# Layers 0, 2 and 3 of a four-layer cross-attention network: projections as 64-row halves in two rounds, values once per quad, a lag of eight waves

## The chip, the core and the metric

The kernel runs on one core of a Trainium2 chip. The metric is device time in microseconds, the median of three runs. The core has TensorE (matrix products, with a queue of its own for weight loads), VectorE, ScalarE, GpSimd and SyncE, which issues most DMAs here. Engines run side by side, each through its own instruction list in order, and wait for one another by semaphores.

## What is computed

x holds 128 rows of 256. Four layers follow, each of cross attention, self attention and a feed-forward part, each added to x. The change touches the cross attention of layers 0, 2 and 3, which has this form (layer 2 has no mask and, like layer 3, an output product):

```python
q = _split_heads(hidden_states @ q_w.T + q_b)      # 128 queries, 16 heads of 16
k = _split_heads(context @ k_w.T + k_b)            # 12544 keys
v = _split_heads(context @ v_w.T + v_b)
scores = jnp.einsum('bhqd,bhkd->bhqk', q, k) / jnp.sqrt(jnp.float32(HD))
scores = jnp.where(mask, -jnp.inf, scores)
probs = jax.nn.softmax(scores, axis=-1)
ctx = jnp.einsum('bhqk,bhkd->bhqd', probs, v)
```

Everything is float32 up to rounding; products that must be exact enough use split high and low parts.

## The kernel before

`cross_attention_turned` (L645) takes the 12544 keys in NB = 14 **blocks** of 896 keys (7 tiles of 128). The softmax is computed block by block with a running maximum. The 16 heads of a block are handled as four **quads** of four heads. A quad takes four **waves**, so a block has 16 waves; I call the four waves of one quad a group and number them 0 to 3 by `g % 4`. One loop over g runs in the lists of TensorE, ScalarE and VectorE; `u = g - LAG` is the wave that has come to its scores when wave g is at its maxima.

What each wave does on TensorE:

- `maxima` (L904 to L917): two products, one for each half of the array's rows (`rows_of(0)` is rows 0 on, `rows_of(1)` rows 64 on), 448 keys wide, into two banks of a ring of three, `m_bank`. VectorE's `top_of` (L1151) reduces each to a row maximum.
- `scores` (L919 to L930): 4 or 3 key tiles, each as two products in the two row halves, into two banks of a second ring of three, `s_bank`. ScalarE's `exps` (L1053) makes `prob` of them, one instruction a bank: four tiles (128x512) or three (128x384).
- `values` (L944 to L955), every second wave, for half a quad: per key tile four products, each with all 128 rows and 32 columns of the array, side by side. They are float32, and each is two instructions in the trace. They sum up in the bank `p_oT`.
- `project_next` (L897), in the other waves: one of the 8 **items** of the next block. Items 0 to 3 are keys (six products of 448 columns each, three split parts times two chunks of the contraction), items 4 to 6 are values for two tiles (twelve products of 256 columns), item 7 for one tile (six). All use all 128 rows, and all go to the one bank `p_proj`. ScalarE copies an item out (`evacuate`, L1037 for keys, L1043 for values), VectorE makes the low part of the keys (`k_low`, L1111).
- `turn_q` once per group: two 128x128 turns of the queries with the new maxima, which VectorE has split in `split_top` (L1175, L1177) out of `raise_top` (L1165). ScalarE copies them to `q_sub` (L1059).
- `turn_out` once per block: four 128x128 turns of the block's result, after ScalarE's `copy_out` (L1071) of 128x512; VectorE adds it up (L1184).

So TensorE's order in a group is maxima, scores, values | maxima, scores, projection, turn of the queries | maxima, scores, values | maxima, scores, projection. In numbers of a block: 16 pairs of maxima, 56 pairs of score products, 56 rounds of four value products, 24 products of 448 and 42 of 256 columns, 8 turns of queries, 4 of the result.

SyncE loads the context of block b + 2 and, once all four key items of block b + 1 are split, rearranges these keys by 24 DMAs, six for each quad, into `k_stack` (L767), where maxima and scores read them. GpSimd splits a loaded context into its parts (L837, and L839 by subtraction). Block 0's projections stand before the loop. The last block has none to make, and after the last maxima LAG more waves of scores, then values and turns, follow before the layer's end.

`keep_busy` (L1240) issues products that nobody uses. The functions that the diff touches, and what calls them:

## Time and profile before

| | us |
|---|---|
| median of 3 runs | 2401.51 |
| lowest, highest | 2388.33, 2405.67 |
| the profiled execution | 2400.72 |
| its span on the core | 2398.9 |
| first to last maxima: layer 0, layer 2, layer 3 | 26.6 to 469.4, 1303.7 to 1741.7, 1831.9 to 2270.0 |

The profile is of one execution. The page lists busy time by engine, the clock granted to TensorE in tenths of the full one, and groups of instructions. The timeline lists runs of like instructions: start, time from the first start to the last end, engine, line, tiles, shape, count. As TensorE's products are pipelined, a run's time is the gaps between the starts and the length of its last product (0.27 us for 128 columns, 0.37 for 448); what follows can start before that end. "128*32" is the part of the array that an instruction uses, rows times columns.

### The profile page before, as it was taken

How to read it: one execution, taken by the hardware profiler on the slowest of the kernel's cores; microseconds unless marked ns; L12 is line 12 of the kernel's file. 1: busy time of each engine (PE TensorE's matmuls, PEld its weight loads, DVE VectorE, ACT ScalarE, POOL GpSimd, SP SyncE). 2: the span in 40 equal slices, each digit the busy share in tenths (PEclk: the TensorE clock that was granted, in tenths of full speed). 3: DMA queues.
4: the chain of work that ended last, by engine and by line, in shares of the span. 5: the costliest groups of instructions: out<-in, count | busy, mean ns of one | idle time of the engine just before them, and what ended most of it. 6: DMA issues, size and time to landing. Idle time of an engine off the chain costs nothing. (4 is left out here: it accounts for less than half of the span.)

```text
span 2398.9 us, 68493 instructions
## 1 busy us (share of the span) xinstructions
PE 2254.4 (94%) x26863; PEld 1884.1 (79%) x26863; DVE 1594.7 (66%) x3621; ACT 1504.3 (63%) x3041; POOL 413.5 (17%) x356
## 2 busy tenths in 40 slices
PE   7999999988999999999778999999977999999968
PEld 6888888777788887887756888888866888888758
DVE  6777777635777777777564777777735777777632
ACT  3666666624788787888524666666633666666611
POOL 3222122002221212210002212222003221122000
PEclk9999999989999999999898999999978999999979
DMA  7667776365344354441154766666516667766335
GB/s 148 118 120 121 125 116 122 54 215 155 100 125 113 106 131 102 116 122 41 46 178 98 148 110 116 115 117 116 82 50 141 121 121 126 127 115 119 57 119 190
DMA packets 152460, 279.62 MB, mean 117 GB/s; under 512 B 32829, under 2 KB 72078, under 8 KB 152218
## 3 DMA queue, kind: packets, MB, share of 16 engines
q1 hardware_dynamic: 148842, 272.18, 55.0%
q10 hardware_dynamic: 3376, 4.03, 0.6%
...
## 5 line engine op out<-in xcount | busy, mean ns | idle before, releaser
L1151 DVE TENSOR_REDUCE L3x_tops<-L3x_m_bank 128x1 f32<-128x448 f32 x448 | 262.6, 619 | 124.5 <-PE L3x_m_bank L915 122.4
L1151 DVE TENSOR_REDUCE L0x_tops<-L0x_m_bank 128x1 f32<-128x448 f32 x448 | 262.7, 619 | 121.8 <-PE L0x_m_bank L915 119.6
L1151 DVE TENSOR_REDUCE L2x_tops<-L2x_m_bank 128x1 f32<-128x448 f32 x448 | 262.7, 619 | 118.4 <-PE L2x_m_bank L915 116.3
L559 DVE CUSTOM_DVE_ANT_0 L1x_p_s<-L1x_p_s,L1x_mask,L1x_neg_max 128x512 f32<-128x512 f32 (+1 forms) x400 | 288.7, 742 | 55.7 <-PE L1x_p_s L320 53.1
L452 ACT ACTIVATE L1x_prob<-L1x_p_s,L1x_neg_max 128x512 f32<-128x512 f32 (+1 forms) x400 | 275.0, 687 | 68.2 <-DVE L1x_neg_max L559 66.2
L1053 ACT ACTIVATE L2x_prob<-L2x_s_bank 128x512 f32<-128x512 f32 x448 | 219.6, 542 | 90.9 <-PE L2x_s_bank L926 89.7
L1053 ACT ACTIVATE L0x_prob<-L0x_s_bank 128x512 f32<-128x512 f32 x448 | 219.6, 542 | 89.9 <-PE L0x_s_bank L926 88.7
L1053 ACT ACTIVATE L3x_prob<-L3x_s_bank 128x512 f32<-128x512 f32 x448 | 219.6, 542 | 87.6 <-PE L3x_s_bank L926 86.1
L329 PE MATMUL L1x_p_t<-net_ident,L1x_prob 128*128 128x128 f32 x1568 | 239.4, 274 | 13.8 <-ACT L1x_probT L174 11.4
L329 PEld LDWEIGHTS L1x_p_t<-net_ident,L1x_prob 128*128 128x128 f32 x1568 | 191.8, 140 | 56.9 <-ACT L1x_probT L174 23.6
L320 PE MATMUL L1x_p_s<-L1x_k_stack,L1x_q_stack 96*128 96x512 f32 (+1 forms) x400 | 181.6, 456 | 1.8 <-DVE L1x_q_stack L542 1.8
L174 ACT COPY L1x_probT<-L1x_p_t 128x512 f32<-128x512 f32 (+1 forms) x300 | 172.7, 576 | 1.6 <-PE L1x_p_t L329 1.3
L926 PEld LDWEIGHTS L2x_s_bank<-L2x_q_sub,L2x_k_stack 50*128 50x128 f32 x1568 | 122.8, 189 | 9.6 <-ACT L2x_prob L1053 6.2
L926 PEld LDWEIGHTS L0x_s_bank<-L0x_q_sub,L0x_k_stack 52*128 52x128 f32 x1568 | 122.5, 188 | 9.4 <-ACT L0x_prob L1053 6.3
L926 PEld LDWEIGHTS L3x_s_bank<-L3x_q_sub,L3x_k_stack 52*128 52x128 f32 x1568 | 121.5, 186 | 9.2 <-ACT L3x_prob L1053 6.1
L926 PE MATMUL L2x_s_bank<-L2x_q_sub,L2x_k_stack 50*128 50x128 f32 x1568 | 116.3, 261 | 3.1 <-ACT L2x_prob L1053 2.9
L926 PE MATMUL L0x_s_bank<-L0x_q_sub,L0x_k_stack 52*128 52x128 f32 x1568 | 115.9, 260 | 3.1 <-ACT L0x_prob L1053 2.9
L926 PE MATMUL L3x_s_bank<-L3x_q_sub,L3x_k_stack 52*128 52x128 f32 x1568 | 114.7, 258 | 3.1 <-ACT L3x_prob L1053 2.9
L915 PE MATMUL L3x_m_bank<-L3x_k_stack,L3x_q_max 52*128 52x448 f32 x448 | 109.1, 467 | 7.3 <-DMA L3x_k_stack<-L3x_kT 5.7
L915 PE MATMUL L0x_m_bank<-L0x_k_stack,L0x_q_max 52*128 52x448 f32 x448 | 109.4, 469 | 4.8 <-DMA L0x_k_stack<-L0x_kT 3.2
L915 PE MATMUL L2x_m_bank<-L2x_k_stack,L2x_q_max 50*128 50x448 f32 x448 | 108.7, 466 | 3.3 <-DMA L2x_k_stack<-L2x_kT 1.6
L953 PE MATMUL L2x_p_oT<-L2x_prob,L2x_v 128*32 128x128 f32 x3136 | 111.6, 281 | 0.0
...
## 6 DMA issues: line engine op xcount, KB each, us to landing
L0x_k_stack<-L0x_kT SPq DMA_DIRECT2D x333, 112.0 KB, 4.1
L2x_k_stack<-L2x_kT SPq DMA_DIRECT2D x333, 112.0 KB, 4.0
L3x_k_stack<-L3x_kT SPq DMA_DIRECT2D x333, 112.0 KB, 4.0
...
```

Source lines behind the costliest of these rows:

```text
L174: copy(probT[:, h % PT_RING, 0:nk], p_t[h % T_RING][:, 0:nk]).then_inc(sem(copied(h)), 1)
L320: e.matmul(p_s[h % S_RING][:, 0:nk], q_stack[0:ROWS, h, :], k_stack[0:ROWS, odd, h // 2, 0:nk], start=True, stop=True).then_inc(sem("score ...
L329: i = e.transpose(p_t[h % T_RING][:, t * P:(t + 1) * P], prob[:, h % P_RING, t * P:(t + 1) * P], ident[:])
L452: e.activation(prob[:, h % P_RING, 0:nk], p_s[h % S_RING][:, 0:nk], ACT.Exp, bias=neg_max[:, odd, h:h + 1], scale=-1.0).then_inc(sem("expe ...
L559: e.tensor_tensor_reduce(s, s, mask[:, odd, 0:nk], -1.0, neg_max[:, 1 - odd, h:h + 1], ALU.add, ALU.min, neg_max[:, odd, h:h + 1]).then_in ...
L915: e.matmul(m_bank[n % RING][:, 0:HALF], q_max[rows_of(r), slot_of(g), :], k_stack[rows_of(r), b % 2, slot_of(g), half * HALF:(half + 1) * ...
L926: mm = e.matmul(s_bank[s_at(u, r) % RING][:, at * P:(at + 1) * P], k_stack[rows_of(r), b % 2, slot_of(u), t * P:(t + 1) * P], q_sub[rows_o ...
L953: mm = e.matmul(p_oT[32 * n:32 * n + VW, j * P:(j + 1) * P], v[:, b % 2, t, n // 2 * 8 + 2 * j + n % 2, :], prob[:, k % 3, n, at, :], star ...
L1053: e.activation(prob[:, k % 3, u % 2 * 2 + r, 0:nt, :].rearrange("p t n -> p (t n)"), s_bank[n % RING][:, 0:nt * P], ACT.Exp).then_inc(sem( ...
L1151: e.tensor_reduce(tops[:, b % 2, h, half:half + 1], m_bank[n % RING][:, 0:HALF], AX, ALU.max).then_inc(sem("m_free"), 1)
```

## The change

- LAG is 8 instead of 7.
- Two banks `p_proj[0]` and `p_proj[1]` take the place of `p_proj` and `p_oT`. The items are made two at a time, as one **pair** per group: x in bank 0 and y in bank 1. Each product is cut into its two halves of 64 rows. In round 0 x uses the upper rows and y the lower, in round 1 the other way round; the products of x and y alternate. Each round is spread over two waves (`third`), next to maxima and scores: round 0 in waves 2 and 3 (in wave 3 between maxima and scores), round 1 in wave 3 and in wave 0 of the next group.
- A quad's values are one series of 28 products in wave 1, right behind the turn of the queries, two groups behind the turn. Both write one bank of the ring `s_bank`. The turn of the result comes between the two, in wave 13 of a block instead of wave 11.
- ScalarE evacuates both items in wave 1 before that wave's exponentials, and copies turned queries and the quad's values (128x128 instead of one 128x512 per block) in wave 2 before that wave's exponentials. The waits on `valued` are gone; the order of ScalarE's own list stands in for them.
- VectorE splits the new maxima before the second reduction of wave 0 instead of after it, and makes the low parts of two key items in wave 1.
- Products without a use: three after each wave's scores once there are no maxima left, three before the last turn of the result, and in the layers with an output product 12 before and 3 between its steps.

The diff, cut to its core (the rest renames banks and semaphores and renumbers the rings):

```diff
@@ -633,7 +633,7 @@
 QUADS = 4
 SLOTS = 8
 WAVES = 16
-LAG = 7
+LAG = 8
...
     m_bank = [ps(f"m_bank{i}") for i in range(RING)]
...
-    p_proj, p_oT = ps("p_proj"), ps("p_oT")
-
-    ITEMS = 8
+    p_proj = [ps(f"p_proj{i}") for i in range(2)]
+
+    ITEMS, PAIRS = 8, 4
...
-    LAST_G = WAVE_END + LAG + 5
...
+    LAST_G = WAVE_END + LAG + 7
+
+    O_WAVE = 13
+    M_BLOCK, M_O = 2 * WAVES + 1, 2 * O_WAVE + 2
...
+    S_GROUP, S_Q = 9, 4
+    S_AT = (0, 2, 5, 7)
+    S_LAST = (NB * QUADS + 1) * S_GROUP
...
+    turned_at = lambda group: group if 0 <= group < NB * QUADS else None
+    valued_at = lambda group: group - 2 if 0 <= group - 2 < NB * QUADS else None
+    def pair_at(group):
+        return (group // PAIRS + 1, group % PAIRS) if 0 <= group < (NB - 1) * PAIRS else None
...
-            def project_next(b, i):
-                if i == 0:
-                    e.wait_ge(sem("ctx_split"), b)
-                if i <= 4:
-                    e.wait_ge(sem("k_split"), 4 * b + i)
-                if i == 0 or i > 4:
-                    e.wait_ge(sem("v_made"), 4 * b + max(i - 4, 0))
-                project(b, i, p_proj)
+            def pair_products(b, i, r, bank):
+                odd, rows = b % 2, half_rows(r)
+                item = 2 * i + bank
...
+                terms = [(wp, cp, c) for wp, cp in PRODUCTS for c in range(DC)]
+                if i < 2:
+                    keys = slice(bank * HALF, (bank + 1) * HALF)
+                    return [(out[:, 0:HALF], wk_part[rows, wp, c, i * P:(i + 1) * P], ctx_part[rows, odd, cp, c, keys])
+                            for wp, cp, c in terms]
+                return [(out[:, n * D:(n + 1) * D], ctx_part[rows, odd, cp, c, t * P:(t + 1) * P], wv_part[rows, wp, c, :])
+                        for n, t in enumerate(v_tiles(item)) for wp, cp, c in terms]
+
+            def project_round(b, i, turn, third):
+                x, y = pair_products(b, i, turn, 0), pair_products(b, i, 1 - turn, 1)
+                if turn == 0:
+                    first, last = (0, 2 * len(x) // 3) if third == 0 else (2 * len(x) // 3, len(x))
+                else:
+                    first, last = (0, len(x) // 3) if third == 0 else (len(x) // 3, len(x))
+                if turn == 0 and first == 0:
+                    if i == 0:
+                        e.wait_ge(sem("ctx_split"), b)
+                        e.wait_ge(sem("v_made"), 4 * b)
+                    elif i < 3:
+                        e.wait_ge(sem("k_split"), 4 * b + 2 * i)
+                    else:
+                        e.wait_ge(sem("v_made"), 4 * b + 2)
+                for k in range(first, last):
+                    if turn and k == 0:
+                        e.wait_ge(sem("half_x_made"), pair_count(b, i))
+                    mm = e.matmul(*x[k], start=turn == 0 and k == 0, stop=turn == 1 and k == len(x) - 1)
+                    if k == len(x) - 1:
+                        mm.then_inc(sem("pair_x_made" if turn else "half_x_made"), 1)
+                    if k < len(y):
+                        if turn and k == 0:
+                            e.wait_ge(sem("half_y_made"), pair_count(b, i))
+                        mm = e.matmul(*y[k], start=turn == 0 and k == 0, stop=turn == 1 and k == len(y) - 1)
+                        if k == len(y) - 1:
+                            mm.then_inc(sem("pair_y_made" if turn else "half_y_made"), 1)
...
             def scores(u):
                 b, half = u // WAVES, u % 4 // 2
                 if u % 4 == 0:
-                    e.wait_ge(sem("s_free"), s_done(s_q_at(u // 4)))
+                    e.wait_ge(sem("q_copied"), u // 4 + 1)
+                if u % 4 == 3 and turned_at(u // 4 + 1) is not None:
+                    e.wait_ge(sem("q_copied"), u // 4 + 2)
...
-            def turn_q(q):
-                n = s_q_at(q)
+            def turn_q(q, bank):
                 e.wait_ge(sem("raised"), 3 * q + 3)
+                for p in range(2):
+                    mm = e.transpose(bank[:, p * P:(p + 1) * P], nat[:, 4 * p + q % 4, :], ident[:])
+                return mm
+
+            def values(q, bank):
+                b, j = q // 4, q % 4
+                if j == 0:
+                    e.wait_ge(sem("v_made"), (b + 1) * 4)
+                for t in range(NT):
+                    for n in range(4):
+                        mm = e.matmul(bank[32 * n:32 * n + VW, 2 * P:3 * P], v[:, b % 2, t, n // 2 * 8 + 2 * j + n % 2, :],
+                                      prob[:, (2 * q + t // 4) % 3, n, t % 4, :], start=t == 0, stop=t == NT - 1)
+                return mm
+
+            def turns_and_values(group):
+                n, q, old = s_q_at(group), turned_at(group), valued_at(group)
                 if n >= S_GROUP:
                     e.wait_ge(sem("s_free"), s_done(n - RING))
                 else:
                     e.wait_ge(sem("v_made"), 4)
-                for p in range(2):
-                    mm = e.transpose(s_bank[n % RING][:, p * P:(p + 1) * P], nat[:, 4 * p + q % 4, :], ident[:])
+                if q is not None:
+                    mm = turn_q(q, s_bank[n % RING])
+                if group % 4 == 2 and group >= 6:
+                    turn_out(group // 4 - 1)
+                if old is not None:
+                    mm = values(old, s_bank[n % RING])
                 mm.then_inc(sem("s_made"), 1)
...
-            def values(k):
...
-                e.wait_ge(sem("s_free"), s_done(s_at(2 * k + 1, 1)))
-                for at, t in enumerate(tiles_of(half)):
-                    for n in range(4):
-                        mm = e.matmul(p_oT[32 * n:32 * n + VW, j * P:(j + 1) * P], v[:, b % 2, t, n // 2 * 8 + 2 * j + n % 2, :],
-                                      prob[:, k % 3, n, at, :], start=t == 0, stop=t == NT - 1)
-                mm.then_inc(sem("valued"), 1)
...
             def turn_out(b):
                 n = m_o_at(b)
-                e.wait_ge(sem("oT_copied"), b + 1)
+                e.wait_ge(sem("s_free"), s_done(s_q_at(4 * b + 3 + 2)))
...
             for g in range(LAST_G):
-                u = g - LAG
+                u, group, wave = g - LAG, g // 4, g % 4
+                pair = pair_at(group - 1 if wave == 0 else group)
...
+                if wave == 3 and pair:
+                    project_round(*pair, 0, 1)
                 if 0 <= u < WAVE_END:
                     scores(u)
-                if u % 2 == 1 and 0 <= (u - 3) // 2 < NB * 8:
-                    values((u - 3) // 2)
-                if u % WAVES == 4 and u > 4:
-                    turn_out(u // WAVES - 1)
-                if g % 2 == 1 and g // WAVES + 1 < NB:
-                    project_next(g // WAVES + 1, g % WAVES // 2)
-                if g % 4 == 1 and 0 <= g // 4 - 1 < NB * QUADS:
-                    turn_q(g // 4 - 1)
+                    if g >= WAVE_END:
+                        keep_busy(e, p_proj[1], ident, 3)
+                if wave == 1 and (turned_at(group - 1) is not None or valued_at(group - 1) is not None):
+                    turns_and_values(group - 1)
+                elif wave == 1 and g // WAVES == NB and g % WAVES == O_WAVE:
+                    keep_busy(e, p_proj[1], ident, 3)
+                    turn_out(NB - 1)
+                if wave == 2 and pair:
+                    project_round(*pair, 0, 0)
+                if wave == 3 and pair:
+                    project_round(*pair, 1, 0)
+                if wave == 0 and pair:
+                    project_round(*pair, 1, 1)
 
             if has_wo:
+                keep_busy(e, p_proj[1], ident, 12)
                 e.wait_ge(sem("o_final"), 1)
                 for c in range(DC):
                     mm = e.transpose(s_bank[0][:, c * P:(c + 1) * P], o[:, c * P:(c + 1) * P], ident[:])
                 mm.then_inc(sem("o2_turned"), 1)
+                keep_busy(e, p_proj[1], ident, 3)
...
-                e.wait_ge(sem("projected"), b * ITEMS + (FIRST_KEYS[i] if b == 0 and i < 4 else i) + 1)
...
+                    e.wait_ge(sem("pair_y_made" if i % 2 else "pair_x_made"), pair_count(b, i // 2))
...
-                    if i == 4 and b >= 2:
-                        e.wait_ge(sem("valued"), 8 * (b - 1))
...
-                if k >= 3 and u % 2 == 0 and r == 0:
-                    e.wait_ge(sem("valued"), k - 2)
...
-            def copy_q(q):
-                n = s_q_at(q)
+            def copy_turned_and_valued(group):
+                n, q, old = s_q_at(group), turned_at(group), valued_at(group)
+                bank = s_bank[n % RING]
                 e.wait_ge(sem("s_made"), s_done(n))
-                e.copy(q_sub[:, q % 4::4, :], s_bank[n % RING][:, 0:2 * P].rearrange("p (s n) -> p s n", s=2)).then_inc(sem("s_free"), 1)
+                if old is None:
+                    e.copy(q_sub[:, q % 4, :], bank[:, 0:P]).then_inc(sem("q_copied"), 1)
+                    e.copy(q_sub[:, 4 + q % 4, :], bank[:, P:2 * P]).then_inc(sem("s_free"), 1)
+                elif q is not None:
+                    e.copy(q_sub[:, q % 4::4, :], bank[:, 0:2 * P].rearrange("p (s n) -> p s n", s=2)).then_inc(sem("q_copied"), 1)
+                if old is not None:
+                    b, j = old // 4, old % 4
+                    if b and j == 0:
+                        e.wait_ge(sem("m_made"), m_done(m_o_at(b - 1)))
+                    e.copy(oT[:, j * P:(j + 1) * P], bank[:, 2 * P:3 * P]).then_inc(sem("s_free"), 1)
...
-            def copy_out(b):
...
-                e.copy(oT[:], p_oT[:]).then_inc(sem("oT_copied"), 1)
...
             for g in range(LAST_G):
-                u = g - LAG
+                u, group, wave = g - LAG, g // 4, g % 4
+                pair = pair_at(group - 1)
+                if wave == 1 and pair:
+                    evacuate(pair[0], 2 * pair[1], p_proj[0])
+                    evacuate(pair[0], 2 * pair[1] + 1, p_proj[1])
+                if wave == 2 and (turned_at(group - 1) is not None or valued_at(group - 1) is not None):
+                    copy_turned_and_valued(group - 1)
                 if 0 <= u < WAVE_END:
                     exps(u, 0)
                     exps(u, 1)
-                if u % WAVES == 2 and u > 2:
-                    copy_out(u // WAVES - 1)
-                if g % 2 == 1 and g // WAVES + 1 < NB:
-                    evacuate(g // WAVES + 1, g % WAVES // 2, p_proj)
-                if g % 4 == 1 and 0 <= g // 4 - 1 < NB * QUADS:
-                    copy_q(g // 4 - 1)
                 if g % WAVES == 4 and g > 4 and g // WAVES - 1 < NB:
                     rise(g // WAVES - 1)
 
...
             for g in range(LAST_G):
-                u = g - LAG
+                pair = pair_at(g // 4 - 1) if g % 4 == 1 else None
+                if g % WAVES == O_WAVE + 1 and g > WAVES:
+                    accumulate(g // WAVES - 1)
                 if g < WAVE_END:
                     top_of(g, 0)
-
-                if g % 2 == 0 and g // WAVES + 1 < NB and 0 < g % WAVES <= 8:
-                    k_low(g // WAVES + 1, g % WAVES // 2 - 1, p_proj)
+                if pair and pair[1] < 2:
+                    k_low(pair[0], 2 * pair[1], p_proj[0])
                 if g % 4 == 0 and 0 < g <= WAVE_END:
                     raise_top(g // 4 - 1)
+                    split_top(g // 4 - 1)
                 if g < WAVE_END:
                     top_of(g, 1)
-                if g % 4 == 0 and 0 < g <= WAVE_END:
-                    split_top(g // 4 - 1)
-                if u % WAVES == 4 and u > 4:
-                    accumulate(u // WAVES - 1)
+                if pair and pair[1] < 2:
+                    k_low(pair[0], 2 * pair[1] + 1, p_proj[1])
```

## Rows read from the trace of the kernel before

**Rows 1.** page, part 1: busy us (share of the span) of each engine.

```profile
PE 2254.4 (94%) x26863; PEld 1884.1 (79%) x26863; DVE 1594.7 (66%) x3621; ACT 1504.3 (63%) x3041; POOL 413.5 (17%) x356
```

**Rows 2.** sums over stretches: PE, PEld, DVE, ACT, POOL busy; clock; DMA.

```profile
188.90:220.70 31.80, 31.80 (x447) 26.84 (x446) 22.81 (x49) 21.93 (x47) 6.76 (x5) 1.00 0.70 121
220.70:253.90 33.20, 32.18 (x447) 27.03 (x446) 24.84 (x49) 22.04 (x47) 6.74 (x5) 1.00 0.74 123
...
445.80:469.40 23.60, 23.22 (x371) 17.54 (x370) 18.29 (x43) 16.71 (x38) 1.04 (x3) 1.00 0.32 48
469.40:490.20 20.80, 13.94 (x204) 10.80 (x200) 3.69 (x11) 8.79 (x19) 0.89 (x2) 0.68 0.01 2
```

**Rows 3.** timeline, TensorE: start, us, line, tiles, count.

```profile
196.78 0.47 PE L915 MATMUL L0x_m_bank<-L0x_k_stack,L0x_q_max 52*128 52x448 f32 x2
197.08 0.56 PE L926 MATMUL L0x_s_bank<-L0x_q_sub,L0x_k_stack 52*128 52x128 f32 x8
197.57 0.86 PE L953 MATMUL L0x_p_oT<-L0x_prob,L0x_v 128*32 128x128 f32 x24
198.36 0.47 PE L915 MATMUL L0x_m_bank<-L0x_k_stack,L0x_q_max 52*128 52x448 f32 x2
198.67 0.45 PE L926 MATMUL L0x_s_bank<-L0x_q_sub,L0x_k_stack 52*128 52x128 f32 x6
199.04 1.48 PE L888 MATMUL L0x_p_proj<-L0x_ctx_part,L0x_wk_part 128*128 128x448 f32 x6
200.36 0.38 PE L940 MATMUL L0x_s_bank<-net_ident,L0x_nat 128*128 128x128 f32 x2
...
203.16 1.51 PE L888 MATMUL L0x_p_proj<-L0x_ctx_part,L0x_wk_part 128*128 128x448 f32 x6
```

**Rows 4.** timeline, TensorE: the rest of the same block.

```profile
188.94 0.48 PE L915 MATMUL L0x_m_bank<-L0x_k_stack,L0x_q_max 52*128 52x448 f32 x2
...
206.87 1.70 PE L893 MATMUL L0x_p_proj<-L0x_wv_part,L0x_ctx_part 128*128 128x256 f32 x12
...
211.20 0.66 PE L962 MATMUL L0x_m_bank<-net_ident,L0x_oT 128*128 128x128 f32 x4
211.62 1.67 PE L893 MATMUL L0x_p_proj<-L0x_wv_part,L0x_ctx_part 128*128 128x256 f32 x12
...
219.82 0.98 PE L893 MATMUL L0x_p_proj<-L0x_wv_part,L0x_ctx_part 128*128 128x256 f32 x6
220.73 0.48 PE L915 MATMUL L0x_m_bank<-L0x_k_stack,L0x_q_max 52*128 52x448 f32 x2
```

**Rows 5.** timeline, TensorE, windows that cut one run of six.

```profile
235.27 1.20 PE L888 MATMUL L0x_p_proj<-L0x_ctx_part,L0x_wk_part 128*128 128x448 f32 x5
...
235.69 0.78 PE L888 MATMUL L0x_p_proj<-L0x_ctx_part,L0x_wk_part 128*128 128x448 f32 x3
```

**Rows 6.** timeline, TensorE in layer 1: turns, then values.

```profile
704.44 0.60 PE L329 MATMUL L1x_p_t<-net_ident,L1x_prob 128*128 128x128 f32 x4
704.98 1.08 PE L345 MATMUL L1x_p_oT<-L1x_probT,L1x_v 128*32 128x128 f32 x32
```

**Rows 7.** timeline, ScalarE: exponentials, evacuation of a key item, copy of queries.

```profile
229.46 1.09 ACT L1053 ACTIVATE L0x_prob<-L0x_s_bank 128x512 f32<-128x512 f32 x2 [0.15 <-PE L0x_s_bank L926]
...
232.35 0.64 ACT L1037 ACTIVATE L0x_kT<-L0x_p_proj,L0x_bias_k 128x448 fp32r<-128x448 f32 x1 [0.54 <-PE L0x_p_proj L888]
232.89 0.36 ACT L1059 CAST L0x_q_sub<-L0x_s_bank 128x256 fp32r<-128x256 f32 x1
```

**Rows 8.** timeline, GpSimd and VectorE in the block from 220.7.

```profile
237.05 4.03 POOL L839 TENSOR_TENSOR L0x_ctx_part<-L0x_ctx,L0x_ctx_part 128x1792 fp32r<-128x1792 f32 x1
...
238.63 2.48 DVE L1175 CAST L0x_nat<-L0x_top 128x4 fp32r<-128x4 f32 x1
```

**Rows 9.** timeline of SyncE's queue, and part 6 of the page.

```profile
206.35 21.01 SPq L767 DMA_DIRECT2D L0x_k_stack<-L0x_kT  x24
...
L0x_k_stack<-L0x_kT SPq DMA_DIRECT2D x333, 112.0 KB, 4.1
```

54 lines of the change are left out of this document (27 added, 27 removed).

## Prediction

> **What bounds the kernel now.** I read four things in this order: the page's busy shares, the sums over one block and over the ends, the timeline of TensorE alone inside one block, and the neighbours that could take over.
>
> TensorE is busy 94% of the span [rows 1]. In a middle block of layer 0 it is busy 31.8 of 31.8 us at the full clock, VectorE 22.8, ScalarE 21.9 and GpSimd 6.8 [rows 2]. Of the 39 blocks with a following block (13 in each of three layers) I count 27 that run 31.8 us to within 0.1, from first maxima to first maxima; so here an instruction stream sets the pace, not a wait.
>
> The stream itself shows what it loses. Six 448-column products take 1.51 us, the last five of them 1.20 and the last three 0.78 [rows 3, 5]: one costs (1.20 - 0.78) / 2 = 0.21 once running, but the first gap is 1.51 - 1.20 = 0.31. 256-column products: (1.70 - 0.98) / 6 = 0.12 each [rows 4]. Scores: (0.56 - 0.45) = 0.11 for one more pair of row halves [rows 3]. Values: (1.08 - 0.86) / 2 = 0.11 for a round of eight instructions, four products that sit side by side [rows 3, 6]. Two 448-column maxima start together in two row halves and are followed by the scores after 0.30, so they run side by side: one after the other they would need 0.42.
>
> Add one block at these running prices: 16 pairs of maxima at 0.207 = 3.3; 56 score pairs at 0.11 = 6.2; 56 rounds of values 6.2; 8 turns of the queries 0.9; 24 key products at 0.207 = 5.0; 42 value-projection products at 0.12 = 5.0; the turn of the output 0.42 (211.20 to 211.62) [rows 4]. Sum 26.9. The block runs from 188.94 to 220.73 = 31.8 [rows 4]. The missing 4.9 lie where TensorE leaves the 64-row form (maxima, scores) for values, projections or turns and comes back: that happens once in each of 16 waves, so **a visit costs 4.9 / 16 = 0.30**. One can see it directly: 24 values occupy 197.57 to 198.36 = 0.79 for 0.66 of work, six key products 1.32 up to the turn for 1.24, and maxima to scores 0.30 for 0.21 [rows 3].
>
> The Trainium skill, "TensorEngine Tiling (Array Packing)", Key Properties, says that changing the tiling mode, other than changing the tile within a mode, drains the engine; it gives no time. By that, the gap at a visit is the drain, and the trace agrees in place (0.30 per visit).
>
> **The change part by part.**
>
> *Projections as halves.* A key item of 6 full-height products becomes 12 half-height ones; two items run as 12 pairs, one per row half. At 0.207 a pair this is 2.48, what two items cost today. No row shows such a pair inside a run; below it is bounded by 0.207 (the full-height product, and the pair cannot stream faster) and above by 0.30 (the maxima pair, entry included). I take 0.207, because the 0.30 also appears as the first gap of a run of single products (0.31) and not at the second: it belongs to entering a form. For 256 columns I take 0.12 likewise; score pairs with 128 columns at 0.11 show that two weight loads per pair fit in that time. The last pair joins items 6 (12 products) and 7 (6): now 18 times 0.12, then 24 times 0.12, as six halves of item 6 in each round have no partner: +0.72 per block.
>
> *Visits.* Projection rounds now have the form of maxima and scores. Only wave 1 of a group leaves it, for turns and values: 4 visits per block, not 16. 12 x 0.30 = 3.6 saved. Inside the visit the form changes once more, from 128x128 turns to 128x32 values: four turns ahead of values take 0.54 (704.44 to 704.98) [rows 6], ahead of a product of their own form 0.42 [rows 4]: 0.12, and somewhat more as the 0.42 holds an entry; I take 0.15, times 4 = 0.6.
>
> Block: 26.9 + 0.7 + 4 x 0.30 + 0.6 = **29.5**.
>
> *Does TensorE then wait?* Follow one key group. In wave 0 it does maxima 0.21, scores 0.44, four pairs 0.83; in wave 1 maxima 0.21, scores 0.44, turns and 14 rounds of values with both gaps about 2.1, then maxima and 0.3: the scores of wave 2 are due 4.5 after the group's start. Their bank needs the second exponential of wave 1. ScalarE can begin wave 0's at 0.9 (scores end plus latency), does 1.09, then both evacuations of 0.64, then 1.09 again [rows 7]: free at 4.4. It just fits. It then has to copy queries (0.36 [rows 7]) and one 128x128 of values, under 0.36, only after the values. At the end of the group, scores of wave 3 are made at 6.8 and the exponential takes half a microsecond more, while wave 0's next scores could start at 7.2: about 0.1 is lost per key group, none in the others, whose rounds are longer (0.48 against 0.41). That is 0.2 per block: **29.7**. VectorE's 22.8 and ScalarE's 21.9 plus 4 smaller copies in place of one stay under 85% of 29.7. The split of the maxima now stands ahead of the second reduction; it is done about 1.7 after the group's start and the turn that waits for it is issued at 2.2, so its wait hides. Maxima behind the values are held up to 2.1, with three banks of VectorE work in front of them; VectorE can idle there, which costs nothing while it has 20% in hand.
>
> *DMAs.* The keys of the next block are complete when the second key pair is split, in wave 1 of group 2: 14.2 + 4.5 = 18.7 into the block. The 24 stacking transfers are issued over 21.0 us [rows 9], the six of the first quad over 5.3, and land 4.1 later [rows 9]: 28.1, ahead of the block's end at 29.7 with 1.6 in hand; today the margin is 14.4 - 9.4 = 5. So I charge nothing, but a block can't get below about 28.
>
> *Ends.* 39 blocks x (31.8 - 29.7) = 82 saved. In each layer the last block has no projections. It takes 23.6, with TensorE 23.2 busy only by overlapping ends [rows 2]; pure work is 16 us, so it is paced by waits between scores, exponentials and banks. With values bunched, the same walk without rounds and evacuations gives 6.5 per group against 5.9: +2.4. One more wave of lag adds 1.1. The tail of 20.8 us ran at a mean clock of 0.68 [rows 2] (levels 1.2 and 2.4 GHz); the added products after each wave keep TensorE occupied and should hold the upper level, worth 2 to 3 us in late values and turns, less about 1.4 for the products themselves where values follow. Net +2.6 per layer, 8 us in all. Start of layer and layer 1 unchanged.
>
> Saving 82 - 8 = 74. Against the profiled execution (2400.7 us, span 2398.9) that gives 2326; its time is within 1 us of the median 2401.5, so **2326** stands for both.
>
> **Rivals.**
>
> *Waits appear, gain halves.* The walk had 0.1 to spare at wave 2. If semaphore latencies or the copies make every group lose 0.4 more, the block is 31.3: 39 x 1.6 = 62 back, about 2385. For it: the last block already shows such waits. Against: a delay in one wave shortens the next wait. Chance 0.13 for 2350 to 2395.
>
> *A half pair costs more than a full product: slower.* The gain per block, 2.1, is spent over 72 pair steps (12 + 12 + 24 + 24) once each costs 0.03 more. At the maxima's 0.30, with 0.1 more on all, the block grows by 7: 2326 + 39 x 7 = 2600. Against: score pairs keep 0.11. Chance 0.06.
>
> A page speaks for it: "TensorE: Matmul & The Clock Gate", Measured speedup vs the span model (Trainium skill), gives 3.07 times for four row tiles, not 4. As an estimate by that page, rounds would take 1.3 times their 10.7 us, +3.2 a block and about 2450. No row here shows a loss of that kind.
>
> *GpSimd holds VectorE's cast.* Today a cast of 0.16 took 2.48 while GpSimd's 4.03 us subtraction ran (from 237.05), and that block took 33.2 instead of 31.8 [rows 2, 8]. That subtraction starts 30.7 after the stacking does [rows 8, 9]. In the changed block: 18.7 + 30.7 - 29.7 = 19.7 to 23.8; the casts come at 15.6 and 23.2. The second is caught for half a microsecond, inside its slack. A shift of 2 us would cost 1 per block (a longer block moves the subtraction earlier, so half of it cancels): 2365. Chance 0.10.
>
> *More than forecast.* If weight loads hide under maxima and rounds, so that each wave's first score pair starts at once, 0.05 per wave or 0.8 per block go too, down to the DMA limit near 28.5: 2285. Chance 0.13.
>
> **Numbers.** Forecast 0.58, own range 2300 to 2350. Faster by over 1% (below 2377, about what a measurement can tell) 0.86: forecast, extra gain, the cast, and most of the waits. Within 1%: 0.06. Slower 0.08: the half pair and what else lengthens a block. Range 2283 to 2370: below lies 0.07, above the rest of the waits and the slower cases.
>
> **What would show it.** Maxima starts 16 waves apart by 29.3 to 30.0; half products in a round 0.207 (keys) and 0.12 (values) per pair; values following turns once per group, some 1.7 long; maxima to scores 0.21 where a round went before, 0.30 after values; ScalarE and VectorE around 75% busy in a block. Wrong, if pairs step by over 0.24; if idle time ahead of scores or maxima with a release by ScalarE, VectorE or a DMA exceeds 0.5 per group; or if casts of over 1 us recur each block.

## The result, and the profile after

| | before | changed |
|---|---|---|
| median, us | 2403.19 (20 runs) | 2389.86 (20 runs) |
| lowest, highest | 2388.33, 2407.61 | 2369.55, 2404.41 |
| ratio of the times | | 0.9948 [0.9931, 0.9965] |
| span of the profiled execution | 2398.9 | 2379.2 |

The change saves 13 us where 74 were forecast: the sign was right, the size was not, and the time lies outside the range. The page of the changed kernel gives busy time by engine, and the clock granted to TensorE in 40 slices of the span:

```profile
PE 2244.4 (94%) x29659; PEld 1942.4 (82%) x29659; DVE 1595.9 (67%) x3621; ACT 1488.4 (63%) x3173; POOL 414.0 (17%) x356
...
PEclk9999999889999999999888999999887999999779
```

TensorE is as busy as before, 94% [rows 1]. From first maxima to first maxima, the blocks of the profiled executions take, in us:

| | block 0 | blocks 1 to 12, median (longest) | last block | last maxima to the addition to x |
|---|---|---|---|---|
| before, layer 0 | 35.0 | 31.8 (33.2) | 23.6 | 19.3 |
| before, layer 2 | 30.3 | 31.8 (33.6) | 23.6 | 24.1 |
| before, layer 3 | 32.3 | 31.8 (32.1) | 23.6 | 19.1 |
| changed, layer 0 | 29.7 | 30.3 (31.2) | 28.4 | 24.9 |
| changed, layer 2 | 29.2 | 30.3 (31.2) | 33.3 | 27.8 |
| changed, layer 3 | 34.5 | 30.3 (31.2) | 33.9 | 24.7 |

A last block is counted to the start of the first of its last two maxima. In the changed kernel the second starts 0.5 to 0.6 later, and the stretches shown below end there.

The 39 blocks with a follower save 57.4 us in sum; the three last blocks give back 24.8; the ends after them give back 14.9; the rest of the span is 2.0 shorter. That is 57.4 - 24.8 - 14.9 + 2.0 = 19.7, the difference of the two spans. Sums over stretches of the changed kernel answer to [rows 2]; the columns are the same. The first line is an undisturbed middle block, the other three hold the last blocks:

```profile
208.70:239.00 30.30, 30.30 (x518) 27.12 (x514) 23.02 (x50) 21.49 (x50) 6.78 (x5) 1.00 0.72 127
423.70:452.70 29.00, 27.58 (x387) 21.38 (x385) 18.16 (x44) 17.89 (x42) 1.04 (x3) 0.88 0.35 54
...
1687.30:1721.20 33.90, 32.95 (x388) 25.32 (x385) 18.39 (x44) 17.84 (x42) 1.03 (x3) 0.70 0.31 47
2214.00:2248.50 34.50, 33.30 (x388) 25.93 (x384) 18.51 (x44) 17.88 (x43) 1.03 (x3) 0.65 0.30 45
```

In the middle block TensorE is busy without a gap at the full clock, in 30.3 us instead of 31.8. In the last blocks the work of VectorE and ScalarE is that of before, but the granted clock has dropped from 1.00 to 0.88, 0.70 and 0.65.

One group inside a middle block (timeline of TensorE: start, us, line, tiles, count) answers to [rows 3, 4]:

```profile
216.10 0.38 PE L958 MATMUL L0x_m_bank<-L0x_k_stack,L0x_q_max 52*128 52x448 f32 x2
216.47 0.66 PE L971 MATMUL L0x_s_bank<-L0x_q_sub,L0x_k_stack 52*128 52x128 f32 x8
...
217.79 0.39 PE L958 MATMUL L0x_m_bank<-L0x_k_stack,L0x_q_max 52*128 52x448 f32 x2
218.00 0.58 PE L971 MATMUL L0x_s_bank<-L0x_q_sub,L0x_k_stack 52*128 52x128 f32 x8
218.51 0.44 PE L980 MATMUL L0x_s_bank<-net_ident,L0x_nat 128*128 128x128 f32 x2
218.88 1.74 PE L989 MATMUL L0x_s_bank<-L0x_prob,L0x_v 128*32 128x128 f32 x56
220.54 0.47 PE L958 MATMUL L0x_m_bank<-L0x_k_stack,L0x_q_max 52*128 52x448 f32 x2
220.85 0.45 PE L971 MATMUL L0x_s_bank<-L0x_q_sub,L0x_k_stack 52*128 52x128 f32 x6
221.13 0.42 PE L939 MATMUL L0x_p_proj<-L0x_ctx_part,L0x_wk_part 64*128 64x448 f32 x1
...
221.40 0.37 PE L939 MATMUL L0x_p_proj<-L0x_ctx_part,L0x_wk_part 64*128 64x448 f32 x1
221.40 0.37 PE L945 MATMUL L0x_p_proj<-L0x_ctx_part,L0x_wk_part 64*128 64x448 f32 x1
221.61 0.37 PE L939 MATMUL L0x_p_proj<-L0x_ctx_part,L0x_wk_part 64*128 64x448 f32 x1
221.61 0.37 PE L945 MATMUL L0x_p_proj<-L0x_ctx_part,L0x_wk_part 64*128 64x448 f32 x1
```

The pairs of halves step by 0.21; only the first step of a round behind scores is longer, 0.27 from 221.13 to 221.40. The one visit to the 128-row form, at 218.51, is entered and left once. Maxima to scores takes 0.21 at 217.79, 0.31 behind the values at 220.54, but 0.37 at 216.10, where 0.21 was forecast and, at the start of a group, a wait of 0.1.

The last block of layer 2, the same view:

```profile
1690.23 1.74 PE L989 MATMUL L2x_s_bank<-L2x_prob,L2x_v 128*32 128x128 f32 x56
1691.89 0.47 PE L958 MATMUL L2x_m_bank<-L2x_k_stack,L2x_q_max 50*128 50x448 f32 x2
...
1693.08 0.46 PE L958 MATMUL L2x_m_bank<-L2x_k_stack,L2x_q_max 50*128 50x448 f32 x1 [0.18 <-DVE L2x_tops L1214]
...
1695.83 0.66 PE L971 MATMUL L2x_s_bank<-L2x_q_sub,L2x_k_stack 50*128 50x128 f32 x8 [0.17 <-ACT L2x_prob L1112]
1696.43 0.52 PE L980 MATMUL L2x_s_bank<-net_ident,L2x_nat 128*128 128x128 f32 x2
1696.88 3.22 PE L989 MATMUL L2x_s_bank<-L2x_prob,L2x_v 128*32 128x128 f32 x56
...
1705.63 3.22 PE L989 MATMUL L2x_s_bank<-L2x_prob,L2x_v 128*32 128x128 f32 x56
```

The values from 1690.23 take 1.74; the same 56 instructions from 1696.88 take 3.22: the clock is at its lower level, 1.2 GHz. Between them TensorE had four waves of maxima and scores with small gaps in between, waiting for a reduction or an exponential. At running prices (four maxima pairs at 0.207, 14 score pairs at 0.11) the 4.5 us from 1691.89 to 1696.43 hold 2.4 of work.

The lower level reaches past the last maxima. The same sums over the end of layer 2 that follows them:

```profile
1720.60:1748.50 27.90, 26.97 (x332) 22.96 (x330) 4.98 (x15) 10.75 (x25) 0.89 (x2) 0.88 0.01 2
```

The ends of layers 0, 2 and 3 ran at a mean clock of 0.86, 0.88 and 1.00.

### The profile page after: what moved, and what is told of

Its sections match the earlier page's. It is cut to its first block and busy times, and to the rows that moved or that the text cites. A ratio compares the mean times of both kernels' runs of the same rounds, so it can differ in the third digit from the quotient of the medians.

```text
span 2379.2 us, 73938 instructions
## 1 busy us (share of the span) xinstructions
PE 2244.4 (94%) x29659; PEld 1942.4 (82%) x29659; DVE 1595.9 (67%) x3621; ACT 1488.4 (63%) x3173; POOL 414.0 (17%) x356
## 5 line engine op out<-in xcount | busy, mean ns | idle before, releaser
L329 PEld LDWEIGHTS L1x_p_t<-net_ident,L1x_prob 128*128 128x128 f32 x1568 | 191.8, 141 | 56.7 <-ACT L1x_probT L174 23.6
L971 PEld LDWEIGHTS L3x_s_bank<-L3x_q_sub,L3x_k_stack 52*128 52x128 f32 x1568 | 128.4, 194 | 20.8 <-issue 16.4
L971 PEld LDWEIGHTS L0x_s_bank<-L0x_q_sub,L0x_k_stack 52*128 52x128 f32 x1568 | 125.3, 189 | 20.4 <-issue 15.5
L971 PE MATMUL L3x_s_bank<-L3x_q_sub,L3x_k_stack 52*128 52x128 f32 x1568 | 134.5, 274 | 1.6 <-ACT L3x_prob L1112 1.5
L971 PE MATMUL L2x_s_bank<-L2x_q_sub,L2x_k_stack 50*128 50x128 f32 x1568 | 132.7, 270 | 2.0 <-ACT L2x_prob L1112 2.0
L971 PE MATMUL L0x_s_bank<-L0x_q_sub,L0x_k_stack 52*128 52x128 f32 x1568 | 131.4, 268 | 2.3 <-ACT L0x_prob L1112 2.2
L958 PE MATMUL L3x_m_bank<-L3x_k_stack,L3x_q_max 52*128 52x448 f32 x448 | 107.3, 414 | 5.1 <-DMA L3x_k_stack<-L3x_kT 4.2
L958 PE MATMUL L0x_m_bank<-L0x_k_stack,L0x_q_max 52*128 52x448 f32 x448 | 105.0, 399 | 4.7 <-DMA L0x_k_stack<-L0x_kT 3.2
L345 PE MATMUL L1x_p_oT<-L1x_probT,L1x_v 128*32 128x128 f32 x3136 | 106.3, 276 | 0.5 <-ACT L1x_probT L174 0.5
```

What stands on the lines that cost most here:

```text
L329: i = e.transpose(p_t[h % T_RING][:, t * P:(t + 1) * P], prob[:, h % P_RING, t * P:(t + 1) * P], ident[:])
L345: i = e.matmul(p_oT[VW * s:VW * s + VW, g * P:(g + 1) * P], v[:, odd, t, h, :], probT[:, h % PT_RING, t * P:(t + 1) * P], start=t == 0, st ...
L958: e.matmul(m_bank[n % RING][:, 0:HALF], q_max[rows_of(r), slot_of(g), :], k_stack[rows_of(r), b % 2, slot_of(g), half * HALF:(half + 1) * ...
L971: mm = e.matmul(s_bank[s_at(u, r) % RING][:, at * P:(at + 1) * P], k_stack[rows_of(r), b % 2, slot_of(u), t * P:(t + 1) * P], q_sub[rows_o ...
```

## The experiments

All edits are to the changed kernel, except where `before` stands in the label. Medians, where given with a ratio, are of 6 to 12 runs, and the ratio is to the kernel before on the same chip. Blocks are compared between single profiled executions.

### Projections full height, in the same places

```diff
-half_rows = lambda r: slice(GROUP * r, GROUP * r + GROUP)
+half_rows = lambda r: slice(0, P)
...
-                x, y = pair_products(b, i, turn, 0), pair_products(b, i, 1 - turn, 1)
+                x = pair_products(b, i, turn, turn)
```

Round 0 now makes item x, round 1 item y, each with all 128 rows.

> The changed kernel, but every projection product uses all 128 rows again, in the same places of the list: round 0 makes item x, round 1 item y, 6 or 12 products instead of 12 or 24 halves in pairs. Everything else as changed. If leaving the 64-row form costs 0.30 a visit, as forecast, four more visits per group (before and after each of the four pieces that stand next to maxima or scores, those of waves 2, 3, 3 and 0) add 4 x 0.30 = 1.2 us to a group of 7.28, and a block grows from 30.3 by 4.8, less 0.7 for item 7 whose products need no idle half: about 34.3. If instead the gain came from how values and waits are placed and the form matters little, the block stays at 29.6 to 30.5.

One run took 2581.81 us, some 190 more than the changed kernel: 39 times 4.0 is 156, and most of the rest are disturbed blocks and longer blocks 0. Undisturbed blocks take 34.3, from 30.3; but others take up to 38.3, and block 0 of layer 2 42.7. An undisturbed stretch, and then a disturbed wave (timeline of TensorE, layer 2):

```profile
1516.68 0.45 PE L964 MATMUL L2x_s_bank<-L2x_q_sub,L2x_k_stack 50*128 50x128 f32 x6
1517.06 1.08 PE L937 MATMUL L2x_p_proj<-L2x_ctx_part,L2x_wk_part 128*128 128x448 f32 x4
1518.07 0.47 PE L951 MATMUL L2x_m_bank<-L2x_k_stack,L2x_q_max 50*128 50x448 f32 x2
...
1525.40 0.66 PE L973 MATMUL L2x_s_bank<-net_ident,L2x_nat 128*128 128x128 f32 x2 [2.58 <-DVE L2x_nat L1233]
```

The lists of VectorE and GpSimd at that turn:

```profile
1521.46 3.59 DVE L1231 CAST L2x_nat<-L2x_top 128x4 fp32r<-128x4 f32 x1
...
1521.02 4.00 POOL L852 TENSOR_TENSOR L2x_ctx_part<-L2x_ctx,L2x_ctx_part 128x1792 fp32r<-128x1792 f32 x1
```

Four products occupy 1517.06 to 1518.07 = 1.01 for 0.83 of work at the running price, and the six scores before them 0.38 instead of 0.28: the visit is back, at each of the 16 pieces of a round in a block. Full-height products save the 0.7 of the unpaired halves, so the 16 visits cost 4.0 + 0.7 = 4.7, or 0.29 each, with what changed in the waits included. So the price of a visit, 0.30, is right, and the forms of the products are what the change gains by. The Trainium skill, "TensorEngine Tiling (Array Packing)", Key Properties, says that changing the tiling mode drains the engine; the trace agrees in place, with 0.29 a visit; that a drain makes up this time is not visible in it. The last row of TensorE shows another thing: a turn that waits 2.58 for VectorE's subtraction (L1233), which stood behind a cast of 3.59 (0.17 elsewhere) beside GpSimd's subtraction of 4.00. All 27 of VectorE's casts that take over 0.3 in this run lie beside that subtraction; of the 16 casts and subtractions that do so in the changed kernel 14 lie beside GpSimd's cast of 1.68, and the longest takes 1.70. So a meeting can cost up to 4 us a block here and 1 there.

The last blocks are the same code as in the changed kernel, and took 25.1, 27.9 and 27.9 here, where there they took 28.4, 33.3 and 33.9. The one of 25.1 ran at a granted clock of 1.00, the others at 0.88.

### Short exponentials

(The indices are shortened; `prob` is also set to zero once, ahead of the loop.)

```diff
-e.activation(prob[..., 0:nt, :], s_bank[n % RING][:, 0:nt * P],
+e.activation(prob[..., 0:2, :], s_bank[n % RING][:, 0:2 * P],
```

> The changed kernel with every exponential over 256 columns instead of 512 or 384; the rest of the probabilities stay zero, so the attention is not the reference's. It takes ScalarE's time per wave from 1.09 and 0.87 to some 0.65 and frees the score banks earlier. In the changed kernel the scores of wave 0 follow the maxima by 0.37 instead of 0.21 while the bank's exponential ends 0.2 before. Theory of the bank wait: maxima to scores falls to 0.21 in every wave 0, a key group from 7.28 to 7.10, a block from 30.3 to 29.7. Rival, that TensorE itself loses this time when it goes from a round to maxima: the block stays at 30.2 or above.

One run took 2380.45. Undisturbed blocks take 29.83, 0.44 less than 30.27, and maxima to scores in wave 0 is 0.27 instead of 0.37 (timeline of TensorE):

```profile
1429.06 0.39 PE L960 MATMUL L2x_m_bank<-L2x_k_stack,L2x_q_max 50*128 50x448 f32 x2
1429.33 0.66 PE L973 MATMUL L2x_s_bank<-L2x_q_sub,L2x_k_stack 50*128 50x128 f32 x8
```

What TensorE waited for stands in the changed kernel's list of ScalarE, one group after the wait at 216.10:

```profile
221.33 0.87 ACT L1112 ACTIVATE L0x_prob<-L0x_s_bank 128x384 f32<-128x384 f32 x2
223.11 0.87 ACT L1112 ACTIVATE L0x_prob<-L0x_s_bank 128x384 f32<-128x384 f32 x2 [0.90 <-PE L0x_s_bank L971]
```

The first of the two from 223.11 takes 0.49, ends at 223.60 and frees the bank; the maxima start at 223.38 and the scores at 223.75, where without a wait they would start at 223.59. ScalarE had been idle for 0.90 before 223.11, so it is not late for lack of capacity: it is fed late. Its scores of wave 3 come behind part of a round, and those of wave 0 follow too soon after. The shorter exponentials took back 0.44 per block, where I had charged 0.2 for such waits; they left 0.06 of 0.16 standing (0.27 for 0.21).

### Filling the last block

(Not shown: before its first unused product the last block waits until the last value item is copied out.)

```diff
+                    if WAVE_END - WAVES + 2 <= g < WAVE_END and wave in (0, 2, 3):
+                        fill_half(2)     # e3: two pairs of 64-row halves, 448 columns
+                        keep_busy(e, p_proj[1], ident, 2)     # e4 instead: two full-height products
```

In both, the products are made behind the scores and nobody uses them. A pair is one product in each row half.

> The changed kernel with two pairs of unused half-height products of 448 columns after the scores in waves 0, 2 and 3 of the last block (from wave 2 on), same form as maxima and scores, no change of form. Clock theory: the last blocks took 28.4, 33.3 and 33.9 us against 23.6 before because the granted clock fell to the 1.2 GHz level between two series of values; with the added work it stays at 2.4 GHz there, the last block takes 24 to 27 in each of the three layers, and the time falls by 15 to 25 us: ratio to before 0.985 to 0.988. Rival, that the bunched values and the waits make the last block slow whatever the clock: the added products only lengthen it, and the ratio is 0.995 to 1.00.

> As the run before, but the added work is two unused full-height float32 products of 128 columns (four instructions) instead of the half-height pairs. They change the form, 0.30 a wave or 3.3 us a layer, so if both kinds hold the clock this one is 5 to 10 us slower than half-height filling; if only products over all rows hold it, the last block shows the 2.4 GHz level here and not there, and this one is faster: ratio 0.987 to 0.990 here, 0.993 or more there.

e3: 2367.09, ratio 0.9859 [0.9826, 0.9891]. e4: 2368.38, 0.9869 [0.9831, 0.9907]. Last blocks 25.7 each in e3 and 27.1 each in e4. e3's last block of layer 2, sums over the stretch and then its timeline of TensorE:

```profile
1685.60:1711.30 25.70, 25.70 (x426) 21.39 (x423) 18.00 (x44) 17.70 (x42) 1.04 (x3) 1.00 0.37 59
```

```profile
1701.57 1.74 PE L996 MATMUL L2x_s_bank<-L2x_prob,L2x_v 128*32 128x128 f32 x56
```

And the sums over the end that follows:

```profile
1711.30:1735.50 24.20, 23.85 (x334) 20.54 (x331) 4.52 (x14) 10.37 (x25) 0.89 (x2) 1.00 0.01 2
```

More work, and 7.6 us less time for it: the clock stays at 1.00, and the values take 1.74 again. So the long last blocks were the clock, and not the walk through exponentials and banks: with the clock held, the block takes 25.7, for which I had forecast 23.6 + 2.4 = 26.0. (e1's block of 25.1 at a clock of 1.00 shows the same without any filling.) The ends gain too: they take 21.3, 24.2 and 24.2 at a clock of 1.00 instead of 24.9, 27.8 and 24.7, 7.6 us in sum, with the same instructions in them. The form of the filling does not matter to the clock; full-height products cost 1.4 more per layer, where I had expected 3.3 for the visits that they bring back, and the two ratios can't be told apart.

### The unused products of the tail

```diff
-                    if g >= WAVE_END:
-                        keep_busy(e, p_proj[1], ident, 3)
...
-                    keep_busy(e, p_proj[1], ident, 3)
...
-                keep_busy(e, p_proj[1], ident, 12)
...
-                keep_busy(e, p_proj[1], ident, 3)
```

> The changed kernel without any of the products that nobody uses in the tail (three a wave, three before the last turn, and the 12 and 3 of the layers with an output product). If they hold the clock as forecast, they were worth 2 to 3 us in a layer and cost 1.4, so the time without them rises by 2 to 6 us: ratio to before about 0.996 to 0.998. Rival: three full-height products a wave, with their change of form, only lengthen the tail (from the last maxima of layer 0 to layer 1 it grew from 20.8 to 22.3 us), and without them the time falls by 3 to 8 us: 0.991 to 0.994.

> The kernel before with only the unused products of the tail added, in the same places (three after each wave's scores once the maxima are done, 12 and 3 in the output part). It does one part of the change alone. Clock theory: the tail of layers 0 and 2, at a mean clock of 0.68 and 0.60 before, goes to 1.0 over most of its length and the time falls by 3 to 8 us, ratio 0.997 to 0.999. Rival: the products delay the scores and values as much as the clock gives back: 0.999 to 1.002.

e5, the changed kernel without them: 2385.81, ratio 0.994 [0.9914, 0.9965]. e6, the kernel before with them: 2402.68, 1.0005 [0.9984, 1.0025]. This part of the change does nothing that can be measured, in either kernel. The profiles show why. Layer 3's tail in the changed kernel, timeline of TensorE:

```profile
2254.70 0.55 PE L971 MATMUL L3x_s_bank<-L3x_q_sub,L3x_k_stack 52*128 52x128 f32 x6
2255.18 0.94 PE L1306 MATMUL L3x_p_proj<-net_ident 128*128 128x128 f32 x6
2256.05 0.55 PE L971 MATMUL L3x_s_bank<-L3x_q_sub,L3x_k_stack 52*128 52x128 f32 x6
...
2260.30 1.74 PE L989 MATMUL L3x_s_bank<-L3x_prob,L3x_v 128*32 128x128 f32 x56
2261.97 0.55 PE L971 MATMUL L3x_s_bank<-L3x_q_sub,L3x_k_stack 52*128 52x128 f32 x6
```

The same in e5:

```profile
2254.05 1.11 PE L971 MATMUL L3x_s_bank<-L3x_q_sub,L3x_k_stack 52*128 52x128 f32 x8 [0.63 <-ACT L3x_prob L1107]
2255.09 3.21 PE L989 MATMUL L3x_s_bank<-L3x_prob,L3x_v 128*32 128x128 f32 x56
```

And in the kernel before:

```profile
2274.40 0.55 PE L926 MATMUL L3x_s_bank<-L3x_q_sub,L3x_k_stack 52*128 52x128 f32 x6 [0.56 <-ACT L3x_prob L1053]
...
2280.14 0.55 PE L926 MATMUL L3x_s_bank<-L3x_q_sub,L3x_k_stack 52*128 52x128 f32 x6 [0.96 <-ACT L3x_prob L1053]
```

In layer 3 the clock is held with the products (values 1.74), but each wave spends 0.87 on them, so that a group takes 7.27 (2254.70 to 2261.97): TensorE has no wait left, and the series of values lies on the path whole. Before, a group of the tail took 5.74 (2274.40 to 2280.14), paced by exponentials, with the values in TensorE's waits. Without the products, e5, the waits are back but the clock falls, and the last two series take 3.21 and 3.22. The two come out alike: last maxima to the addition to x takes 24.9, 27.8, 24.7 with them and 24.0, 28.5, 27.2 without. In the kernel before it takes 19.2, 22.1 and 22.1 with them, at a clock of 1.00, and 19.3, 24.1 and 19.1 without. Nor do the products always hold the clock: in layers 0 and 2 of the changed kernel it fell for 6.8 us behind the last maxima. They were not taken out of a kernel whose last block is filled, so what they are worth there is not known.

### Filling the start too

```diff
+                if 2 <= g < 8:
+                    for _ in range(4):
+                        for r, bank in ((0, s_bank[0]), (1, s_bank[2])):
+                            e.matmul(bank[:, 0:D], wk_part[half_rows(r), HIGH, 0, 0:P], wk_part[half_rows(r), HIGH, 1, :],
+                                     start=True, stop=True)
```

> The changed kernel with the half-height filling of the last block (ratio 0.9859 before this), and in the first block of each layer, in waves 2 to 7 where no scores run yet, four pairs of unused half-height products of 256 columns each, some 0.5 us a wave. First blocks took 29.2 us where the clock stayed up and 32 to 34.5 where it fell. If the fall comes from thin work in these waves, all first blocks take 29.5 to 30.5 and the time falls by a further 3 to 8 us: 0.983 to 0.985. Rival: the clock falls because of the wait before the first maxima, or VectorE sets the pace there; then the ratio stays at 0.985 to 0.987.

This is on top of e3. 2368.56, ratio 0.9869 [0.9843, 0.9896]: no gain on e3. The blocks 0 took 34.2, 29.5 and 36.2, as long as in other runs; the clock still falls in the two long ones (0.90 and 0.86, against 1.00). This filling was not what block 0 lacks, and what it lacks stays open.

### GpSimd's long instructions cut up

```diff
-                e.tensor_copy(ctx_part[:, odd, HIGH], ctx[:]).then_inc(sem("ctx_high"), 1)
+                for c in range(DC):
+                    for half in range(2):
+                        keys = slice(half * HALF, (half + 1) * HALF)
+                        i = e.tensor_copy(ctx_part[:, odd, HIGH, c, keys], ctx[:, c, keys])
+                i.then_inc(sem("ctx_high"), 1)
```

The subtraction is cut likewise. e8 has this and e3's filling, e10 this alone, e9 has it in the kernel before.

> The changed kernel with the half-height filling of the last block, and GpSimd's cast (1.68 us) and subtraction (4.03) of the context each cut into four instructions of 448 columns. In about half of the blocks VectorE's cast or subtraction of the maxima lasts as long as the GpSimd instruction beside it, and these blocks take 30.6 to 31.4 us instead of 30.3. If VectorE gets its turn between two pieces, no such instruction lasts over 1.2 us, all middle blocks take 30.3 to 30.5 and the time falls by 8 to 14 us: ratio 0.980 to 0.983. Rival: GpSimd keeps the way for the whole series of pieces, or the pieces meet more VectorE instructions: 0.986 or above.

> The kernel before with only GpSimd's cast and subtraction of the context cut into four instructions each. Its profile shows 36 middle blocks that lose 6 us to such stalls in all. If that is all the cutting can give, ratio 0.996 to 0.998; if part of the changed kernel's gain from the cut came because the new order meets GpSimd more often, the gain here is smaller than the 0.6% there. Rival: equal gain, 0.993 to 0.995, then the collisions are no matter of the change.

> The changed kernel with the cut GpSimd work alone, no filling of the last block. If the two repairs are independent, the ratio is that of the changed kernel (0.9948) less the step from filled to filled and cut (0.9859 to 0.9796): 0.988 to 0.990. Last blocks stay at 28 to 34 us with the clock at the 1.2 GHz level in parts, middle blocks at 30.3. Rival: filling the last block matters less once the stalls are gone, 0.982 to 0.985.

| ratio to the kernel before | not cut | cut |
|---|---|---|
| kernel before | 1 | 0.9976 [0.9952, 1.0001] (e9) |
| changed | 0.9948 [0.9931, 0.9965] | 0.9886 [0.9845, 0.9928] (e10) |
| changed, last block filled | 0.9859 [0.9826, 0.9891] (e3) | 0.9796 [0.9769, 0.9824] (e8) |

The cut is worth 0.6% of the changed kernel in either row, known to about 0.4%, and 0.24% before, where the interval touches 1. The filling is worth 0.9% in either column, known to about as much. e8's median is 2349.47, and it beats both kernels. The mechanism, in the changed kernel's timeline of the block from 1443.8, which takes 31.2 instead of 30.3:

```profile
1459.64 0.17 DVE L1238 CAST L2x_nat<-L2x_top 128x4 fp32r<-128x4 f32 x1
...
1459.85 1.68 POOL L850 CAST L2x_ctx_part<-L2x_ctx 128x1792 fp32r<-128x1792 f32 x1 [5.74 <-DMA L2x_ctx<-in_ctxT]
1459.85 1.70 DVE L1240 TENSOR_TENSOR L2x_nat<-L2x_top,L2x_nat 128x4 fp32r<-128x4 f32 x1
...
1461.69 0.41 PE L980 MATMUL L2x_s_bank<-net_ident,L2x_nat 128*128 128x128 f32 x2 [0.79 <-DVE L2x_nat L1240]
```

A subtraction of 0.17 takes 1.70 while GpSimd's cast runs, and the turn waits for it. In e8, where a like pair meets (lists of VectorE, then GpSimd):

```profile
224.67 0.29 DVE L1257 CAST L0x_nat<-L0x_top 128x4 fp32r<-128x4 f32 x1
225.00 0.46 DVE L1259 TENSOR_TENSOR L0x_nat<-L0x_top,L0x_nat 128x4 fp32r<-128x4 f32 x1
```

```profile
224.38 2.08 POOL L853 CAST L0x_ctx_part<-L0x_ctx 128x448 fp32r<-128x448 f32 x4 [5.25 <-DMA L0x_ctx<-in_ctxT]
```

The two are held for 0.12 and 0.29 instead of for the length of the whole. Where a short instruction meets a piece of the subtraction, it can still take up to 1.19, beside pieces of 1.14 and 1.16. Leaving out each layer's block 0, the 36 others exceed 30.3 by 7.7 us in sum in the changed kernel, by 13 in e3, and by 1.4 in e8. In the kernel before they exceed 31.8 by 5.7, and with the cut (e9) still by 5.3: there the profiles show no gain in the blocks. The Trainium skill, "SBUF — State Buffer", Who interferes with whom, says that VectorE and GpSimd share a pair of ports, that a VectorE instruction with two inputs in SBUF, as this subtraction, contends for it with a GpSimd instruction that reads SBUF, and that whoever issues first has the pair for the whole instruction while the other blocks. The traces agree: 1.70 beside a cast of 1.68, 0.46 here beside pieces of 2.08 / 4 = 0.52, and about the length of a piece at most in e8.

### Less filling, and another tail

```diff
-                        fill_half(2)
+                        fill_half(1)     # e11, on top of e8
...
-                        keep_busy(e, p_proj[1], ident, 3)
+                        fill_half(2)     # e12, on top of e8: in the waves of the tail
```

> Cut GpSimd work, and one pair of unused half-height products in waves 0, 2 and 3 of the last block instead of two. If one pair is enough to hold the clock, the last block takes 24.3 to 25.4 us in place of 25.7, and the ratio is 0.978 to 0.980. If the amount of added work decides, the clock falls in some last blocks, which then take 27 to 34, and the ratio is 0.981 to 0.986.

> Cut GpSimd work, two pairs in the last block, and in the tail two pairs of half-height products after each wave's scores in place of three full-height ones, so that the form does not change there. If the change of form costs 0.30 a wave, eight waves and three layers give back up to 5 to 7 us where TensorE sets the tail's pace: ratio 0.977 to 0.979. Rival: ScalarE's exponentials set that pace, no change within 2 us: 0.979 to 0.981.

e11: 2357.17, ratio 0.9802 [0.9764, 0.984]. e12: 2355.51, 0.98 [0.9764, 0.9837]. Neither can be told from e8. One pair in each of the three waves, 0.21 us at the running price, was enough to hold the clock of the last block in the profiled run: 25.5 in all three layers. But e11's tails of layers 0 and 2 took 24.7 and 27.6, with e8's at 21.3 and 24.2: there the clock fell soon behind the last maxima, to a mean of 0.86 and 0.88. So its 0.2 per block is not seen in the time. Half-height products in the tail give tails of 19.9 to 22.8 (e8: 21.3 to 24.2) in the profiled runs, but blocks 0 were longer there.

## Why the prediction was off, step by step

**Prices of pairs: right.** 0.207 for 448 columns was exact (221.40 to 221.61), 0.12 for 256 columns likewise, and weight loads hid. The longer first step of 0.27 is made up by the scores ahead of it, six in 0.28 where 0.33 was charged. The rival of the dear half pair fell, and with it its estimate of 2450: two row halves side by side ran at twice one's rate, without loss. The 0.72 for item 6's unpaired halves was right as well. A row half with nothing to do does go on by itself (timeline of TensorE, changed kernel):

```profile
240.34 0.47 PE L958 MATMUL L0x_m_bank<-L0x_k_stack,L0x_q_max 52*128 52x448 f32 x1
...
240.81 0.36 PE L958 MATMUL L0x_m_bank<-L0x_k_stack,L0x_q_max 52*128 52x448 f32 x1
```

But that saves nothing, as the turn at 241.50 needs both: from the scores at 239.31 to it pass 2.19 us, and the prices give 2.05.

**A visit at 0.30, four instead of sixteen: right.** e1 made 16 more of them and lost 4.0 per block, 34.3 - 30.3, or 4.7 without what it saves on unpaired halves: 0.29 each.

**Waits at 0.2 per block: 0.36 too small, and the work of wave 0 by another 0.2.** I placed one wait, at the start of a group, for the bank of wave 3's first exponential, and sized it 0.1 in two groups of a block. It is 0.16 at 216.10, and all four groups have it: maxima to scores in the four waves 0 of the block from 208.71 takes 0.33, 0.37, 0.37 and 0.31, in sum 0.56 over the price. e2 took 0.44 of it back. The other 0.2 is no wait: in wave 0 eight scores and four pairs take 1.33 (216.47 to 217.79, and the same in e2), where the prices give 1.27. What makes this up stays open. The block came to 30.27 instead of 29.7: 0.57 x 39 = 22 us of the miss. Blocks 0 and disturbed blocks make it 82 - 57.4 = 24.5. The rival of appearing waits named this mechanism, at 1.6 per block; it has about a quarter of that.

**The last block at +2.4: right for the walk, wrong for the clock.** I had the clock on the list for the tail alone, and let the last block run at the full one since [rows 2] show 1.00 for it. But I had also said that bunching the values leaves waits between the series. In the kernel before, values fall in every second wave; changed, there are four waves of half-empty work between two series, and the clock fell there in all three layers. The three blocks cost 24.8 instead of 7.2: 17.6 us of the miss. e3 shows that it was the clock: filled, 25.7; and e1's block of 25.1 at the full clock shows it without filling.

**The tail at +0.2 net: wrong by 14.** It grew by 5.6, 3.7 and 5.6 instead. Two steps failed. The added products "should hold the upper level"; in layers 0 and 2 they did not, behind a last block that had lost it, and e3's tails at a clock of 1.00 take 7.6 less in sum. And I put 1.4 on the unused products "where values follow" and took the other waves for waits. There, 0.87 a wave was more than the wait of 0.56 to 0.96 it replaced, once the values too were in the way. The gain of the clock that I counted is real where it comes, values at 1.74 for 3.21, but it is all spent: e5 and e6 show that the products are worth nothing net. The rest, from e6's 63.3 in three tails to e3's 69.8 with the products and the clock at 1.00 in both, is the added wave and the bunched values: 6.5, for which 3.3 was charged. This division is rough, since it adds up single profiles, and the tail of layer 0 of the kernel before took 19.3 in one and, with the clock held, 15.7 in another (e9).

**GpSimd and VectorE: named, and under-rated.** The rival asked when the subtraction falls on the cast, and worked out a meeting "inside its slack". The subtraction's time of arrival varies with the load of the context (GpSimd waited for it 5.74 at 1459.85), so the meeting is not fixed, and GpSimd's cast holds VectorE's subtraction as well. In the profiled runs disturbed blocks cost about 6 us before and 8 after; the cut saved 0.6% of the changed kernel, some 15 us, known to about 10. The profiles account for 6 of them (e10) and 12 (e8).

In sum 24.5 + 17.6 + 14.3 = 56.4 us fewer were saved; the rest of the span, for which I charged nothing, was 2.0 shorter. That is the 54 between the forecast of 74 and the 20 of the profiled pair. The median gained 6 less than that pair. The runs of the changed kernel spread over 35 us, those of before over 19, and blocks and tails of the same code differ from profile to profile with the clock, so I put the 6 down to it; that is argued, not shown.

**Open.** Why block 0 takes 28 to 36 us in any kernel (in e1 up to 43); e7's filling did not settle it. What makes wave 0 0.06 longer than its prices. And whether a tail can keep the clock for less than its waits: e12 could not be told from e8.
